# Attention and mixture of experts in one core: a shorter way from quotient to logits, four routing groups instead of five

## The chip, the cores and the metric
The kernel runs on one core of a Trainium2 chip. The metric is the device time of one execution in microseconds. Before the change three runs gave 344.79, 345.01 and 345.48 us, median 345.01. The engines are PE (matrix multiplication), DVE (vector), ACT (scalar), POOL (general purpose, which here also issues the indirect DMAs) and SP (which issues the other DMAs).

## What is computed
A block of two layers on 16 sequences of 256 tokens with 128 channels, all in float32 as far as the result shows:

```python
x = x + attn(layernorm(x))        # causal linear attention, 16 heads of 8: phi(q), phi(k) = elu + 1
#   kv = running sum of k outer v, ksum = running sum of k; y = (q kv) / (q ksum + 1e-6); y @ W_proj + b
x = x + moe(layernorm(x))         # 8 experts, hidden width 512, top 2 of a softmax over x @ Wr + br
#   h = relu(x @ W1[e] + b1[e]); out = h @ W2[e] + b2[e]; mixed with the two normalised gates
```

## The kernel before, in words
**Stages.** First the projections q, k, v of all 16 sequences are made (up to 47.6 us of the profile). Then a loop over s = 0 to 15 makes the attention of one sequence (two tiles of 128 tokens) a step. A last stage runs the experts over 39 blocks of 256 token slots; behind it the rows are gathered, mixed with the gates and stored.

**A step of the loop.** All engines are programmed by hand, each with its own order of instructions, and meet at semaphores. PE makes running sums of k outer v by matrices of ones (`prefix(s+1, 0)` and `prefix(s+1, 1)`), single-buffered in PSUM, so each waits until DVE has multiplied the former content (`multiply`, L923). DVE multiplies by q, reduces over a head (`reduce`, L934) and divides (`quotient`, L942 to L946). PE turns the quotient (`turn_y`, L1305), ACT copies it out (`copy_yT`, L645), PE projects it (`proj`, L1313 to L1317). ACT copies the new x with its sum (`copy_x2`, L651) and makes variance (`statistics(s-1)`); POOL raises it to the power -1/2 (`power_2`, L524); ACT scales x (`norm_2`, L672 to L690); PE turns that (`turn_x2(s-3)`, L1327), ACT copies it (`copy_x2T`, L697), and PE makes the router's logits (`logits(s-3)`, L1337).

**Routing.** Sequences are routed in groups of `GROUPS`. When the logits of a group are complete, DVE chooses the two experts of each token (`choose_first`, `choose_second`, 15 small operations), PE ranks them (`ranks`) and DVE makes `positions`. With these POOL scatters the rows of each half tile to the regions of their experts in DRAM (`scatter_x`, L534, 64 in all); after a block of experts it scatters two outputs (`scatter_y`, L566, 78 in all). After the first three groups (10 sequences) DVE works out a table of blocks (`table_*`), which PE spreads over partitions (`spread`) and DVE copies (`table_copies`, L1083).

**Weights.** Scales of the expert weights are made on DVE (`scales`). ACT casts the weights to a high part in two passes (`cast_weights`, L639, 32 calls), POOL subtracts for the low part (`weights_low`, 16). Tables give how many of these stand in which step: `CASTS` (between the copies, behind them), `LOWS`, `KV_AT` (products of k and v on POOL), `X_AT` (row scatters).

## Time and profile before

| | us |
|---|---|
| median of 3 runs | 345.01 |
| the profiled execution | 345.68 |
| its span | 343.93 |
| PE busy | 289.6 (84%) |
| DVE busy | 275.0 (80%) |
| ACT busy | 224.7 (65%) |
| POOL busy | 248.5 (72%) |
| granted TensorE clock, mean | 0.936 |

Between the profiled execution and the span lie 1.75 us, and the profiled execution is 0.67 us over the median. Busy shares are means over stages with different limits, so the sections below read the stages one by one. The loop's steps are best counted by the start of L946, the last operation of a quotient: it comes once a step.

### The profile page before, as it was taken

The numbers are of one execution on the slowest core, as the hardware profiler recorded it, in microseconds if no ns is written. First come the engines' busy times: TensorE is split into PE (matmuls) and PEld (weight loads), VectorE is DVE, ScalarE is ACT, GpSimd is POOL, SyncE is SP. The second block draws the span as 40 slices with busy tenths as digits, with TensorE's granted clock in tenths as the row PEclk, the third lists the DMA queues.
The fourth block names the chain that finished last, engine by engine and source line by source line (L and its number), as shares of the span: only waits on it lengthen the run. The fifth ranks groups of instructions, "written<-read, shape, count | busy, mean of one in ns | idle before, by whom it ended". The sixth has DMA issues, their size and how long they took to land.

```text
span 343.9 us, 7875 instructions
## 1 busy us (share of the span) xinstructions
PE 289.6 (84%) x2234; PEld 207.3 (60%) x2237; DVE 275.0 (80%) x623; ACT 224.7 (65%) x654; POOL 248.5 (72%) x252
## 2 busy tenths in 40 slices
PE   4798999989989999899695799999999999995000
PEld 4587855545545555555453577688888898884000
DVE  5888899999978987997999279986777777773096
ACT  2588721469989855555408896688888888882091
POOL 4648999659999998877775577777777777777200
PEclk9699999999999999999879699999999999999655
DMA  8991000000000001011110364516445645511497
GB/s 226 352 286 47 0 2 0 0 4 0 1 0 2 0 15 43 31 53 50 42 51 33 78 110 103 104 56 102 110 104 105 117 99 104 98 56 53 134 381 240
DMA packets 50026, 29.16 MB, mean 85 GB/s; under 512 B 34993, under 2 KB 44639, under 8 KB 49986
## 3 DMA queue, kind: packets, MB, share of 16 engines
q1 hardware_dynamic: 45142, 19.02, 22.6%
q0 software_dynamic: 4544, 9.38, 9.4%
q8 instruction: 20, 0.33, 0.4%
q10 hardware_dynamic: 300, 0.27, 0.3%
q14 instruction: 20, 0.16, 0.2%
HBM read 10.87 MB, written 12.67 MB: 68 GB/s over the span
## 4 chain that ended last, share of the span: by engine, by line
PE 43%; DVE 19%; ACT 12%; POOL 10%; issue 10%; DMA 4%; SPq 1%; ACTq 0%; POOLq 0%; DVEq 0%
POOL y_rows L566 10%; PE ps L1286 9%; PE ps L1285 6%; PE ps L1259 4%; DVE nd L934 3%; ACT xs L682 3%; DMA qk<-y_rows 3%; PE ps L1449 2%; PE ps L1261 2%; PE ps L1451 2%; PE ps L1450 2%; PE ps L1468 2%; PE ps L1473 2%; PE ps L1469 2%; ACT junk L661 2%
## 5 line engine op out<-in xcount | busy, mean ns | idle before, releaser
L566 POOL DMA_INDIRECT y_rows<-kvt,yid x78 | 74.7, 957 | 23.8 <-issue 22.3
L534 POOL DMA_INDIRECT x_rows<-rows,pos_i x64 | 62.4, 974 | 21.3 <-issue 17.4
L740 ACT ACTIVATE ps<-ps,b1s 128x256 f32<-128x256 f32 x156 | 60.1, 448 | 16.9 <-PE ps L1451 16.2
L1171 DVE TENSOR_TENSOR wraw<-ps,wraw 128x1024 f16<-128x1024 f32 x39 | 47.8, 1225 | 19.9 <-ACT wraw L746 19.6
L1449 PE MATMUL ps<-wraw,w1h 128*128 128x256 f16 x156 | 43.4, 278 | 0.5 <-issue 0.4
L1451 PE MATMUL ps<-wraw,w1l 128*128 128x256 f16 x156 | 43.1, 276 | 0.0
L1450 PE MATMUL ps<-wraw,w1h 128*128 128x256 f16 x156 | 43.1, 276 | 0.0
L934 DVE TENSOR_REDUCE nd<-work 128x144 f32<-128x1152 f32 x32 | 41.9, 1348 | 0.4
L923 DVE TENSOR_TENSOR work<-ps,qk 128x1024 f32<-128x1024 f32 x32 | 38.1, 1216 | 5.0 <-PE ps L1286 4.9
L1468 PE MATMUL ps<-w,wraw 128*128 x312 | 39.8, 219 | 0.0
L1469 PE MATMUL ps<-w,wraw 128*128 x312 | 39.7, 219 | 0.0
L645 ACT ACTIVATE xT_s<-ps 128x256 f32<-128x256 f32 x16 | 6.1, 381 | 41.2 <-PE ps L1305 41.1
L1468 PEld LDWEIGHTS ps<-w,wraw 128*128 128x128 f16 x312 | 30.1, 97 | 0.9 <-issue 0.2
L1469 PEld LDWEIGHTS ps<-w,wraw 128*128 128x128 f16 x312 | 30.3, 97 | 0.2
L1166 DVE CAST wraw<-ps 128x512 f16<-128x512 f32 x39 | 26.9, 690 | 2.9 <-ACT ps L740 2.6
L746 ACT ACTIVATE wraw<-ps 128x512 f16<-128x512 f32 x39 | 23.3, 597 | 3.6
L505 POOL TENSOR_TENSOR kvt<-qk,v 128x1024 f32<-128x1024 f32 x12 | 25.3, 2135 | 0.0
L1473 PE MATMUL ps<-w,wraw 128*128 x312 | 23.8, 219 | 0.2 <-DVE wraw L1171 0.2
L1286 PE MATMUL ps<-kvt,tri 128*128 128x512 f32 x48 | 23.6, 593 | 0.0
L1259 PE MATMUL ps<-wqkv,xT_s 128*128 128x256 f32 x64 | 20.4, 403 | 0.0
L1449 PEld LDWEIGHTS ps<-wraw,w1h 128*128 x156 | 15.4, 98 | 7.3 <-issue 3.9
L1473 PEld LDWEIGHTS ps<-w,wraw 128*128 128x128 f16 x312 | 19.0, 98 | 0.5 <-DVE wraw L1171 0.4
(250 smaller groups left out, 733.1 us busy)
## 6 DMA issues: line engine op xcount, KB each, us to landing
qk<-y_rows SPq DMA_DIRECT2D x8, 512.0 KB, 6.7
wraw<-in_L_ffn_W_dram SPq DMA_DIRECT2D x1, 2048.0 KB, 11.1
out_dram<-x SPq DMA_DIRECT2D x8, 256.0 KB, 4.3
x<-in_L_attn_x_dram SPq DMA_DIRECT2D x3, 512.0 KB, 7.2
y_rows<-kvt,yid POOLq DMA_INDIRECT x78, 2.8
x_rows<-empty SPq DMA_DIRECT2D x9, 130.0 KB, 2.8
x_rows<-rows,pos_i POOLq DMA_INDIRECT x64, 2.3
wraw<-x_rows SPq DMA_TRANSPOSE x39
```

The lines of the kernel that those rows point to most:

```text
L534: nc.gpsimd.indirect_dma_start(out=x_rows, out_offset=bass.IndirectOffsetOnAxis(ap=pos_i[:, c, t:t + 1], axis=0), in_=rows[:, t, :], in_of ...
L566: nc.gpsimd.indirect_dma_start(out=y_rows, in_=ysb[:, n % YG, g], in_offset=None, out_offset=bass.IndirectOffsetOnAxis(ap=yid[:, n, g:g + ...
L740: ins = nc.scalar.activation(o, o, ACT.Relu, bias=b1s[:, bass.ds(e * HC + c, 1)])
L934: nc.vector.tensor_reduce(nd[:, s % 2, a].rearrange("p (h j) -> p j h", j=NPL), m_s[:, a].rearrange("p (j h i) -> p j h i", j=NPL, i=DH), ...
L1171: nc.vector.tensor_tensor(hl[:, n % HB], inner(n), hh[:, n % HB], ALU.subtract).then_inc(lo_done, 1)
L1286: ins = nc.tensor.matmul(o, tri[:, :], kv[a][:, cols], start=(a == 0), stop=True)
L1449: nc.tensor.matmul(o, wh, xh, start=True, stop=False)
L1450: nc.tensor.matmul(o, wh, xl, start=False, stop=False)
L1451: ins = nc.tensor.matmul(o, wl, xh, start=False, stop=True)
L1468: nc.tensor.matmul(o, h, second_layer(n, c, 0), start=False, stop=False)
L1469: nc.tensor.matmul(o, h, second_layer(n, c, 1), start=False, stop=False)
L1473: ins = nc.tensor.matmul(o, hl[:, n % HB, c, g * P:(g + 1) * P], second_layer(n, c, 0), start=False, stop=(g == GPB - 1 and c == HC - 1))
```

## The change
1. The turn of the normed x, the logits and all that follows come one step earlier: `norm_2(s-1)`, `turn_x2(s-2)`, `logits(s-2)` instead of s-2, s-3, s-3. `turn_x2` now stands behind both prefixes of PE, the logits behind the denominators. ACT copies x2T at the end of its step, ahead of the casts, not at its start.
2. Four groups of 5, 5, 3 and 3 sequences instead of five of 3, 4, 3, 3 and 3. A group is chosen three steps after its last sequence (`ROUTE`) instead of four; group 2, whose like was chosen behind the loop, is chosen in step 15. The table is still of the first 10 sequences and made in steps 12 to 14 instead of 13 to 15.
3. The weights' scales are made in step 0 instead of 1, `bias_scales` in step 1 instead of 2. The casts stand in steps 0, 1 and 3 to 6 (11, 5, 4, 4, 4, 4) instead of 2 to 7 (6 each, then 2).
4. Intermediate values of scales and of the choice lie in PSUM instead of SBUF, and some buffers are shared.

```diff
-    GROUPS = [3, 4, 3, 3, 3]
+    GROUPS = [5, 5, 3, 3]
-    FIRST = 3
+    FIRST = 2
+    ROUTE = 3
+    TABLE_AT = G_LAST[FIRST - 1] + ROUTE
-    CASTS = {**{s: (3, 3) for s in range(2, 7)}, 7: (2, 0)}
-    LOWS = {3: 3, 4: 3, 5: 3, 6: 3, 7: 3, 8: 1}
+    CASTS = {0: (4, 7), 1: (0, 5), 3: (0, 4), 4: (0, 4), 5: (0, 4), 6: (0, 4)}
+    LOWS = {0: 4, 1: 1, 2: 2, 3: 1, 4: 2, 5: 2, 6: 4}
-    KV_AT = {0: (6, 7), 2: (8,), 3: (9,), 4: (10,), 5: (11,), 6: (12,), 7: (13,), 8: (14,), 10: (15,)}
+    KV_AT = {0: (6, 7), 1: (8,), 2: (9,), 3: (10,), 4: (11,), 5: (12,), 6: (13,), 11: (14, 15)}
-    X_AT = {8: 2, 9: 5, 10: 5, 11: 6, 12: 6, 13: 4, 14: 9, 15: 3}
+    X_AT = {7: 5, 8: 5, 9: 5, 10: 5, 12: 8, 13: 6, 14: 6}
+    X_LATE = 2
...
@@ POOL, a step of the loop
-                if s == 2:
-                    pool.wait_ge(scale_done, 1)
-                if s >= 2:
-                    power_2(s - 2)
+                if s >= 1 and s < U - 1:
+                    power_2(s - 1)
...
@@ POOL, behind the loop
+            for n in range(sent, sent + X_LATE):
                 scatter_x(n)
-            last_group = TOP * TPU * G_U0[NG - 1]
             power_2(U - 2)
-            scatter_x(TOP * T1)
+            for n in range(sent + X_LATE, sent + 2 * X_LATE + 1):
+                scatter_x(n)
             power_2(U - 1)
...
@@ ACT, a step of the loop
             for s in range(U):
-                if s >= 3:
-                    copy_x2T(s - 3)
-                if s - 3 in ended_by:
-                    copy_logits(ended_by[s - 3])
                 between, behind = CASTS.get(s, (0, 0))
                 for n in range(cast, cast + between):
                     cast_weights(n)
                 copy_yT(s)
+                if s - 2 in ended_by:
+                    copy_logits(ended_by[s - 2])
                 if s >= 1:
                     statistics(s - 1)
                 copy_x2(s)
...
-                if s >= 2:
-                    norm_2(s - 2)
+                if s >= 1:
+                    norm_2(s - 1)
+                if s == U - 1:
+                    statistics(s)
+                if s >= 1:
+                    copy_x2T(s - 1)
                 for n in range(cast + between, cast + between + behind):
                     cast_weights(n)
...
@@ DVE, a step of the loop
-                if s == 3:
+                if s == 0:
+                    maxima_over_partitions()
+                if s == 1:
+                    bias_scales()
                     second_sides()
-                if s == 1:
-                    maxima_over_partitions()
-                if s - 4 in ended_by:
-                    choose_first(ended_by[s - 4])
-                    choose_second(ended_by[s - 4])
+                if s - ROUTE in ended_by:
+                    choose_first(ended_by[s - ROUTE])
+                    choose_second(ended_by[s - ROUTE])
                 reduce(s, 0)
...
+                if s == 0:
+                    scales()
+                if s == U - 1:
+                    positions(FIRST)
                 reduce(s, 1)
-                if s == U - 1:
+                if s == TABLE_AT + 2:
                     table_copies(0)
                 quotient(s)
...
-                if s >= 3:
-                    split_low(s - 3)
+                if s >= 2:
+                    split_low(s - 2)
...
-            choose_first(FIRST)
-            choose_second(FIRST)
-            positions(FIRST)
-            split_low(U - 3)
             split_low(U - 2)
...
@@ PE, turn_y(u)
-                if u >= 3:
-                    pe.wait_ge(x2T_out, u - 2)
+                if u >= 2:
+                    pe.wait_ge(x2T_out, u - 1)
...
@@ PE, a step of the loop
                 if s + 1 < U:
                     prefix(s + 1, 0)
...
-                if s == U - 1:
+                if s + 1 < U:
+                    prefix(s + 1, 1)
+                if s >= 2:
+                    turn_x2(s - 2)
+                if s == TABLE_AT + 2:
                     pe.wait_ge(x2_done, s)
                     spread(0)
-                if s >= 3:
-                    turn_x2(s - 3)
-                if s + 1 < U:
-                    prefix(s + 1, 1)
-                if s - 4 in ended_by:
-                    ranks(ended_by[s - 4])
-                elif s == U - 1:
-                    pe.wait_ge(table_done, 2)
-                    logits(s - 3)
-                elif s >= 3:
-                    logits(s - 3)
+                if s - ROUTE in ended_by:
+                    ranks(ended_by[s - ROUTE])
                 turn_y(s)
                 if s + 1 < U:
                     prefix_denominators(s + 1)
...
+                if 2 <= s < U - 1:
+                    logits(s - 2)
+                if s - 2 in ended_by:
+                    pe.wait_ge(lg_out, ended_by[s - 2] + 1)
                 proj(s)
...
@@ PE, behind the loop
-            pe.wait_ge(x2T_out, U - 3)
-            ranks(FIRST)
-            pe.wait_ge(rank_out, FIRST + 1)
-            turn_x2(U - 3)
             logits(U - 3)
             turn_x2(U - 2)
             up(0)
```

**On PE, a step without a choice.** Before, from the first prefix of a step to the denominators (xs is the normed x, xsT its turned copy, y_s the quotient):

```order
L1286 MATMUL ps<-kvt,tri 128x512 [waits m_done,kv_done]
L1286 MATMUL ps<-kvt,tri 128x512
L1327 MATMUL ps<-ident,xs 128x128 [waits x2T_out,yT_out,xs_done]
L1327 MATMUL ps<-ident,xs 128x128
L1285 MATMUL ps<-kvt,ones 128x512 [waits m_done,kv_done]
L1286 MATMUL ps<-kvt,tri 128x512
L1285 MATMUL ps<-kvt,ones 128x512
L1286 MATMUL ps<-kvt,tri 128x512
L1337 MATMUL ps<-wr,xsT 128x8 [waits small_in3,x2_done,x2T_out]
L1337 MATMUL ps<-wr,xsT 128x8
L1305 MATMUL ps<-ident,y_s 128x128 [waits x2T_out,yT_out,y_done]
L1305 MATMUL ps<-ident,y_s 128x128
```

With the change the same stretch, up to the logits, reads (L1296 and L1297 are the prefixes, L1338 the turn of x2, L1316 the turn of y, L1350 the logits):

```order
L1297 MATMUL ps<-rows,tri 128x512 [waits m_done,kv_done]
L1297 MATMUL ps<-rows,tri 128x512
L1296 MATMUL ps<-rows,ones 128x512 [waits m_done,kv_done]
L1297 MATMUL ps<-rows,tri 128x512
L1296 MATMUL ps<-rows,ones 128x512
L1297 MATMUL ps<-rows,tri 128x512
L1338 MATMUL ps<-ident,xs 128x128 [waits x2T_out,yT_out,xs_done]
L1338 MATMUL ps<-ident,xs 128x128
L1316 MATMUL ps<-ident,y_s 128x128 [waits x2T_out,yT_out,y_done]
L1316 MATMUL ps<-ident,y_s 128x128
L1305 MATMUL ps<-qk,tri 128x128 [waits y_done,m_done]
L1306 MATMUL ps<-qk,tri 128x128
```

The turn of x2 has moved from between the prefixes to right ahead of the turn of y, and that one's wait on x2T_out is now for ACT's copy of this same x2.

**On ACT, between two steps with casts.** Before, from the last part of a norm to the statistics of the next step (w2 and wraw are the weights, L639 a cast):

```order
L690 ACTIVATE ps<-xs 128x256 [waits xl_done]
L639 ACTIVATE wraw<-wraw,sc 128x512 [waits pfx_done,scale_done]
L639 ACTIVATE w2<-wraw,sc 128x4x128 [waits pfx_done,scale_done]
L639 ACTIVATE wraw<-wraw,sc 128x512 [waits pfx_done,scale_done]
L697 ACTIVATE xsT<-ps 128x256 [waits lg_done,x2T_done]
L639 ACTIVATE w2<-wraw,sc 128x4x128 [waits pfx_done,scale_done]
L639 ACTIVATE wraw<-wraw,sc 128x512 [waits pfx_done,scale_done]
L645 ACTIVATE xT_s<-ps 128x256 [waits proj_done,yT_done]
L657 ACTIVATE mean<-sums 128x2 [waits x2_done]
```

With the change (L701 ends the norm, L708 is the copy of x2T, L647 a cast, L653 the copy of yT):

```order
L701 ACTIVATE ps<-xs 128x256 [waits xl_done]
L708 ACTIVATE xsT<-ps 128x256 [waits lg_done,x2T_done]
L647 ACTIVATE w2<-wraw,sc 128x4x128 [waits pfx_done,scale_done]
L647 ACTIVATE wraw<-wraw,sc 128x512 [waits pfx_done,scale_done]
L647 ACTIVATE w2<-wraw,sc 128x4x128 [waits pfx_done,scale_done]
L647 ACTIVATE wraw<-wraw,sc 128x512 [waits pfx_done,scale_done]
L653 ACTIVATE xT_s<-ps 128x256 [waits proj_done,yT_done]
```

The copy of x2T has moved ahead of all casts that stand between two steps, and four of them lie between it and the copy of yT.

## Rows read from the trace of the kernel before

**Rows 1.** Busy time by stretch: the loop (us, busy of PE, PEld, DVE, ACT, POOL).
```profile
47.56:185.32 137.76, 126.39 (x528) 71.35 (x526) 126.03 (x249) 80.79 (x283) 115.12 (x95) 0.98 0.06 19
```

**Rows 2.** The chain that ended last, one step of it (start, us, what).
```profile
119.32 0.86 PE ps L1285 x2
...
127.46 0.86 PE ps L1285 x2
```

**Rows 3.** Timeline of DVE: the quotients of steps 0, 3, 7, 11 and 15.
```profile
55.56 0.42 DVE L946 TENSOR_TENSOR y_s<-nd,ps 128x256 f32<-128x256 f32 x1
...
79.28 0.42 DVE L946 TENSOR_TENSOR y_s<-nd,ps 128x256 f32<-128x256 f32 x1
...
113.21 0.42 DVE L946 TENSOR_TENSOR y_s<-nd,ps 128x256 f32<-128x256 f32 x1
...
146.87 0.42 DVE L946 TENSOR_TENSOR y_s<-nd,ps 128x256 f32<-128x256 f32 x1
...
184.90 0.42 DVE L946 TENSOR_TENSOR y_s<-nd,ps 128x256 f32<-128x256 f32 x1
```

**Rows 4.** Timeline of PE, from the logits of step 7 to step 8.
```profile
114.45 0.51 PE L1337 MATMUL ps<-wr,xsT 128*128 128x8 f32 x4
114.81 0.41 PE L1305 MATMUL ps<-ident,y_s 128*128 128x128 f32 x2
...
115.74 0.60 PE L1313 MATMUL ps<-x,ident 128*128 128x256 f32 x2
...
116.28 0.61 PE L1317 MATMUL ps<-wproj,xT_s 128*128 128x128 f32 x4
116.73 1.88 PE L1286 MATMUL ps<-rows,tri 128*128 128x512 f32 x4
118.88 0.44 PE L1327 MATMUL ps<-ident,xs 128*128 128x128 f32 x2 [0.27 <-ACT xs L682]
```

**Rows 5.** Timeline of ACT: copy of x2T, casts, copy of yT.
```profile
113.19 0.36 ACT L697 ACTIVATE xsT<-ps 128x256 f32<-128x256 f32 x1
113.45 0.71 ACT L639 ACTIVATE w<-wraw,sc 128x512 f16<-128x512 f32 x1
114.06 0.71 ACT L639 ACTIVATE wraw<-wraw,sc 128x512 f32<-128x512 f32 x1
115.27 0.39 ACT L645 ACTIVATE xT_s<-ps 128x256 f32<-128x256 f32 x1 [0.50 <-PE ps L1305]
```

**Rows 6.** DVE: the products' group with its waits, and one choice's ends.
```profile
L923 DVE TENSOR_TENSOR work<-ps,qk 128x1024 f32<-128x1024 f32 x30 | 35.7, 1216 | 5.0 <-PE ps L1286 4.9
...
132.56 0.22 DVE L983 TENSOR_TENSOR ps<-lg,ps 128x64 f32<-128x64 f32 x1
...
136.37 2.61 DVE L934 TENSOR_REDUCE nd<-work 128x144 f32<-128x1152 f32 x2
```

**Rows 7.** Timelines of PE and DVE around the table.
```profile
171.08 3.75 PE L1286 MATMUL ps<-wraw,tri 128*128 128x512 f32 x4 [2.86 <-DVE work L923]
...
179.46 0.51 PE L1337 MATMUL ps<-wr,xsT 128*128 128x8 f32 x4
...
183.94 0.17 DVE L1083 CAST table_i<-ps 128x26 int32<-128x26 f32 x1
```

**Rows 8.** Timeline of POOL: the 41st row scatter and the last.
```profile
191.52 1.03 POOL L534 DMA_INDIRECT x_rows<-rows,pos_i  x1 [3.15 <-DVE rows L954]
192.58 0.72 POOL L524 TENSOR_TENSOR rstd<-var,neghalf 128x2 f32<-128x2 f32 x1
...
319.85 0.96 POOL L566 DMA_INDIRECT y_rows<-kvt,yid  x1 [0.31 <-issue]
```

**Rows 9.** The reduces of a choice, from PSUM and from SBUF, by form.
```profile
L968 DVE TENSOR_REDUCE r<-ps 128x6 f32<-128x48 f32 x6 | 1.2, 207 | 0.2
L968 DVE TENSOR_REDUCE r<-ps 128x8 f32<-128x64 f32 x2 | 0.5, 225 | 0.1
...
201.60 0.20 DVE L968 TENSOR_REDUCE r<-lg 128x6 f32<-128x48 f32 x1
```

More of the change, by code:

```diff
@@ L211, in block_kernel @@
         ps_br = scratch(E)
+        ps_sc = scratch(10)
         ps_lg = scratch(MOST, E)
-        ps_others = scratch(MOST, E)
         ps_second = scratch(MOST, E)
         ps_xs = ps[:, 5, 0:TPU * D].rearrange("p (a d) -> p a d", a=TPU)
+        ps_wall = ps[:, 6, T + P:T + P + 3]
+        b2s, b2f = (ps[0:E, 5, TPU * D + k * D:TPU * D + (k + 1) * D] for k in range(2))
         def kv_home(u):
@@ L371, in routed @@
         def routed(g, at, n):
-            if g > FIRST or g == FIRST and at >= RANK:
+            if g > FIRST or g == FIRST and at >= COUNT:
                 return ps[:, 6, at:at + n]
@@ L545, in _ @@
             for s in range(U):
-                if s == 2:
-                    pool.wait_ge(scale_done, 1)
-                if s >= 2:
-                    power_2(s - 2)
-                for n in range(low, low + LOWS.get(s, 0)):
+                if s >= 1 and s < U - 1:
+                    power_2(s - 1)
+                for n in range(low, low + LOWS.get(s, 0) if s else 0):
                     weights_low(n)
-                low += LOWS.get(s, 0)
                 for u in KV_AT.get(s, ()):
                     kv_products(u)
-                if s in (5, 10):
-                    token_ids(s // 10)
+                if s == 0:
+                    for n in range(LOWS[0]):
+                        weights_low(n)
+                low += LOWS.get(s, 0)
+                if s in (3, 9):
+                    token_ids(s // 9)
                 for n in range(sent, sent + X_AT.get(s, 0)):
-                    assert G_LAST[in_group[n // TOP // TPU]] + 5 <= s
+                    assert G_LAST[in_group[n // TOP // TPU]] + ROUTE <= s
                     scatter_x(n)
@@ L674, in norm_2 @@
                 act.wait_ge(shift2_done, u + 1)
-                if u == U // 2:
-                    act.wait_ge(pfx_done, 10 * TPU)
+                if u in (0, U // 2):
+                    last = max(w for w in range(U) if KV_HOME[w] == f"rows{u // (U // 2)}")
+                    act.wait_ge(pfx_done, (last + 1) * TPU)
                 if u >= 4:
@@ L754, in copy_y @@
                                      ACT.Copy).then_inc(y_out, 1)
-            statistics(U - 1)
-            copy_x2T(U - 3)
-            norm_2(U - 2)
-            copy_x2T(U - 2)
             norm_2(U - 1)
@@ L885, in scales @@
             def scales():
[L886 removed]
+                piece = lambda a, b: ps_sc[:, a:b]
+                i32 = lambda a, b: ps_sc[:, a:b].bitcast(I32)
                 EXPONENT = 0x7F800000
[L888 to L891 removed]
@@ L898, in scales @@
[L898 to L908 removed]
+                dve.wait_ge(wall_done, 1)
@@ new lines, in scales @@
+                link(nc.vector.tensor_scalar(piece(0, 2), ps_wall[:, 0:2], 1e-18, None, ALU.max))
+                link(nc.vector.tensor_scalar(i32(2, 4), i32(0, 2), EXPONENT, None, ALU.bitwise_and))
+                link(nc.vector.tensor_copy(sc[:, 6:7], ps_wall[:, 2:3]))
+                link(nc.vector.scalar_tensor_tensor(out=piece(4, 5), in0=piece(2, 3), scalar=2.0 * D, in1=sc[:, 6:7],
+                                                    op0=ALU.mult, op1=ALU.add))
+                link(nc.vector.tensor_scalar(i32(5, 6), i32(4, 5), EXPONENT, None, ALU.bitwise_and))
@@ new lines, in scales @@
+                link(nc.vector.reciprocal(piece(6, 7), piece(5, 6)))
+                link(nc.vector.reciprocal(piece(7, 8), piece(3, 4)))
+                link(nc.vector.tensor_scalar(sc[:, 13:14], piece(7, 8), W_TOP, None, ALU.mult))
+                link(nc.vector.tensor_scalar(sc[:, 17:18], piece(6, 7), H_TOP, None, ALU.mult))
+                nc.vector.tensor_scalar(sc[:, 12:13], piece(6, 7), H_TOP / X_SCALE, None, ALU.mult).then_inc(scale_done, 1)
+            def bias_scales():
+                piece = lambda a, b: ps_sc[:, a:b]
+                link(nc.vector.scalar_tensor_tensor(out=piece(8, 9), in0=piece(7, 8), scalar=W_TOP, in1=sc[:, 17:18],
+                                                    op0=ALU.mult, op1=ALU.mult))
+                link(nc.vector.tensor_copy(sc[:, 19:20], piece(8, 9)))
+                link(nc.vector.reciprocal(sc[:, 20:21], piece(8, 9)))
+                dve.wait_ge(small_in[6], 16)
+                link(nc.vector.tensor_scalar(b2s, b2r[:, :], sc[0:E, 19:20], None, ALU.mult))
+                link(nc.vector.tensor_copy(b2hml[:, 0], b2s))
+                link(nc.vector.tensor_tensor(b2f, b2s, b2hml[:, 0], ALU.subtract))
+                link(nc.vector.tensor_copy(b2hml[:, 1], b2f))
+                nc.vector.tensor_tensor(b2hml[:, 2], b2f, b2hml[:, 1], ALU.subtract).then_inc(b2_done, 1)
```

91 lines of the change are left out of this document (36 added, 55 removed).

## The prediction, made before the changed kernel was run
> **What bounds the kernel now.** I read the busy time by stretch first [rows 1]: in the loop over 16 sequences (47.56 to 185.32 us) DVE is busy 126.0 and PE 126.4 of 137.8 us, so either may bind. The chain that ended last and the engines' timelines then say where. Behind the loop it is POOL: from its 41st row scatter (191.52) to the last (319.85) stand 101 pitches and one power_2 [rows 8], which is 1.26 us a scatter and no wait between, and 23.1 us of gather, mix and store follow to the span's 343.93. So the end is the moment at which POOL gets its 41st row scatter, plus a fixed tail. That scatter waits for the positions of group 3, which DVE works out after the loop's last quotient (184.90). So what the loop's last quotient loses or wins goes whole to the end, and the distance from it to the last scatter (319.85 - 184.90 = 134.95 us) is the second term.
>
> Inside the loop the steps take 6.7 us where DVE alone binds, and 8.14 where the chain goes round through PE and ACT (119.32 to 127.46) [rows 2]. PE's own work in such a step [rows 4], start to start: logits 0.36, turn of y (0.26) and denominators (0.67) 0.93, projection 0.54 + 0.45, first prefix 1.72, turn of x2 an estimated 0.28 of its 0.44, second prefix 3.44 (four of 0.86; the chain's first such piece is in [rows 2]): 7.7 us. So PE can't follow DVE's 6.7; it catches up only where DVE makes a choice. DVE waits 5.0 us in all for prefixes, 1.0 in the step shown [rows 6]. A part of it is PE's stop of 0.27 for ACT's xs, ahead of the second prefix.
>
> **The change, part by part.** All steps are counted from quotient to quotient (start of L946) [rows 3]: before has 55.56, then 23.72 for steps 1 to 3, 33.93 for 4 to 7, 33.66 for 8 to 11 and 38.03 for 12 to 15.
>
> *The turn of x2 behind the second prefix.* This takes ACT's xs off the way to the prefix. But the turn of y of step s now waits for x2T_out of s-2, and the turn that feeds it is the instruction right ahead of it; before, 3.44 us of prefix lay between. From start to start: turn 0.44, ACT's copy 0.38, two semaphores of 0.05 make 0.92 instead of 0.27 [rows 4, 5]. So PE's step is 7.7 + 0.65 = 8.35 us, and the way before took 8.14. The hoped-for gain (PE free of the xs wait) is spent at once, and the denominators, behind the turn of y, come 0.7 us late to DVE as well.
>
> *Casts.* ACT now has four casts (0.61 each) between the copy of x2T (s-1) and the copy of yT (s+1), in steps 3 to 6, and the copy of x2T waits for PE's turn behind the second prefix. That closes a ring: projection's last part 0.45, prefixes 5.16, turn 0.44, copy 0.28, casts 2.45, copy of yT 0.38, semaphores 0.1: 9.26 us a step [rows 2, 4, 5]. Before, three casts stood there and PE's second prefix covered them. DVE follows the ring: split_low waits about 1.8 us for xs_beside, whose norm is in the step of ACT that is late. Steps 4 to 6: 3 x 9.26 = 27.8. Step 7 holds the choice of 10 tiles: 6.7 + choice 4.05 (3.81 for 8 tiles [rows 6], and 15 operations by 0.018 for 16 elements more, as the reduce of 48 and of 64 shows, 0.207 and 0.225 [rows 9]) + waits of 1.85 (split_low), 0.7 (denominators) and 1.3 (the copy of logits stands behind casts and copy of yT) = 14.6. Less 0.4 that the first ring finds ready: 42.0 against 33.93, **+8.1 us**.
>
> *Steps 0 to 3.* Step 0 takes the maximum and ten scale operations of 0.2 us: +2.0. Steps 1 to 3 lose them and take one split_low (0.33) earlier: -1.5. Together **+0.5 us**.
>
> *Steps 8 to 11.* They lose a choice (before in step 10). PE starts them caught up by the choice of step 7, so two go at about 7.3 and two at 8.35. Once POOL is late: its last weights_low wait for the casts of step 6, two kv_products stand behind them, and power_2(6) is needed in the same step now, not one later; ACT stands about 4 us and split_low 2.9. 7.3 + 9.6 + 7.3 + 8.35 = 32.5 against 33.66: **-1.2 us**.
>
> *Steps 12 to 15.* Step 12: the larger choice, +0.5, and waits of 0.9 and 0.7 where before had about 1.2 of its 5.0 in that stretch: +0.4. The group that was chosen after the loop is chosen in step 15: 3.81 - 0.26 = 3.55 for 6 tiles, and two operations for its positions, 0.5 in all. And the table is read one step earlier, in step 14, where PE still has two prefixes ahead of spread. The trace prices that [rows 7]: in before PE gets the table step's first product at 171.08 and has the second prefix done at 179.46, for a part at 1.2 GHz (four matmuls take 3.75 us where the step in [rows 4] has 1.88). The same stretch, then turn of y with its wait 0.91, denominators, logits and projection 2.0, prefixes 5.16, turn 0.27 and spread 0.5, comes to 188.3; DVE from the same point is at table_copies after 183.94 - 171.08 = 12.9. It waits some 4.2 us; before it waited nothing, since step 15 has no prefix to make. Sum 0.5 + 0.4 + 4.1 + 4.2 = 9.2, with 0.2 of late denominators: 47.4 against 38.03, **+9.4 us**.
>
> The last quotient so comes 16.8 us late, at 201.7. Walking all engines through both orders with these durations gives 16.2 (and for before a loop of 129.9 us where the trace has 129.3); I take 16.5.
>
> *After the loop.* The 41st scatter needed the choice behind the loop and came 6.6 us after the quotient (191.52). Its positions are now there before the quotient; POOL, still at the scatters of step 14, takes it 1.5 us after. In its stream stands one power_2 more (1.0), a wait for var(15) (0.4), and one of 1.85 for y_out(1), since PE starts its first block 7.4 instead of 8.8 us after the quotient. Last scatter: quotient + 1.5 + 127.6 + 2 x 1.0 + 1.3 = +132.4, against 134.95: **-2.5 us**. PE is not the bound: its last copy of y (316.21, 122.5 after block 0 starts at 193.69) would be 129.9 after the quotient and allow +131.6.
>
> *Into PSUM.* Scale chain and marks move from SBUF to PSUM. The same reduce of 48 takes 0.21 from PSUM and 0.20 from SBUF [rows 9], so I cost it at nothing: 0 to 0.01 x 40 operations = 0.4 us. The Trainium skill, "VectorE: DVE Perf Modes", section on the TRN2 errata, gives 58 cycles of fixed cost from SBUF and 120 from PSUM at 0.96 GHz; by that the sum would be an estimated 2.6 us more for 40 operations. The rows here don't bear that out.
>
> Sum: +16.5 - 2.5 = **+14.0 us** on the profiled 345.68, so 359.7; the median of before is 0.67 lower, so **359.0**.
>
> **Rivals.** (1) *Clock stays up.* The 2.86 us of idle ahead of 171.08 came with the half clock [rows 7]. In after, PE stands about 3 us in step 13. If it doesn't fall, 3 us of the 4.2 of table_copies go, less what then waits for y: 356.7. For it: that idle is at the edge. 15 in 100. (2) *The casts hide*, if ACT is free before PE needs yT: then 8.35 instead of 9.26 for four steps, 355.3. Against it: the waits are in order. 9 in 100. (3) *Faster.* If the turn of y finds x2T ready and ACT keeps up, only DVE binds: the 5.0 us for prefixes [rows 6] go, 1.9 of added DVE work comes (two larger choices, one split_low, positions in the loop), and 2.5 go after the loop: 345.0 - 3.1 - 2.5 = 339.4. It decides where the 0.65 us per step is nought and the four casts don't stand ahead of yT. For it: DVE's work fits; against it: two instructions side by side on PE with ACT between. 6 in 100. (4) *Worse.* power_2 is late in most steps, since it must come between var and norm_2 of one ACT step now and takes 0.72 [rows 8]; if POOL's scatters (1.26 each, five to eight a step) stand ahead of it in steps 8 to 14, another 1 us a step: 366. 8 in 100. (5) *No change* within 0.2% (what a measurement of this kernel can tell): 2 in 100.
>
> **How the numbers follow.** The forecast has 60 in 100, between 357 and 362. With (1) and half of (2) the range reaches down to 354.5, and up to 362.5: 8 in 10. Faster 0.06, same 0.02, slower 0.92.
>
> **What would show it.** Quotients 9 us and more apart in steps 4 to 6, with four casts between copy of x2T and copy of yT; PE idle 0.65 us for x2T at the turn of y in every step; DVE idle of 4 us ahead of table_copies and of over 1 us ahead of split_low; the 41st scatter within 2 us of the last quotient. The forecast is wrong if split_low and the turn of y don't wait, or if DVE's idle in the loop stays near 6 us.

## The result, and the profile after

Four runs of the changed kernel take 363.4 to 366.2 us, median 364.38, beside 344.79 to 345.56 (median 345.25, four runs) for the kernel before: ratio 1.056 (95% interval 1.051 to 1.061). The forecast was 359.0 in a range of 354.5 to 362.5: the right direction and too little of it. The profiled execution took 363.4 us, span 361.7, so in the span the change costs 17.8 us, where the working has 14.0.

The page of the changed kernel, its busy times and the clock in 40 slices. PE, DVE, ACT and POOL do almost the work of before. What is new is idle time, and more of the lower clock around the table and behind the loop: 0.66 in the 20th slice (172 to 181 us), 0.68 and 0.50 in the 23rd and 24th (199 to 217 us). Before, the lowest of these were 0.67 in 171 to 180 us and 0.62 in 189 to 198 us:

```profile
PE 293.0 (81%) x2232; PEld 210.3 (58%) x2235; DVE 275.4 (76%) x606; ACT 226.7 (63%) x653; POOL 248.6 (69%) x252
...
PEclk9899999999999999999699658999999999999755
```

The quotients of steps 0, 3, 7, 11 and 15, for [rows 3]:

```profile
57.48 0.42 DVE L962 TENSOR_TENSOR y_s<-nd,ps 128x256 f32<-128x256 f32 x1
...
79.80 0.42 DVE L962 TENSOR_TENSOR y_s<-nd,ps 128x256 f32<-128x256 f32 x1
...
121.93 0.42 DVE L962 TENSOR_TENSOR y_s<-nd,ps 128x256 f32<-128x256 f32 x1
...
156.16 0.42 DVE L962 TENSOR_TENSOR y_s<-nd,ps 128x256 f32<-128x256 f32 x1
...
204.83 0.42 DVE L962 TENSOR_TENSOR y_s<-nd,ps 128x256 f32<-128x256 f32 x1
```

The same stretches by engine (us, busy of PE, PEld, DVE, ACT, POOL with instructions in brackets, clock). In steps 4 to 7 DVE works 30.9 of 42.1 us and the clock is full, so engines wait for each other there; only behind 121.93 does the clock take part:

```profile
79.80:121.93 42.13, 37.26 (x156) 20.82 (x154) 30.92 (x52) 28.56 (x95) 30.20 (x23) 1.00 0.00 1
121.93:156.16 34.23, 30.57 (x124) 18.29 (x125) 27.38 (x39) 19.74 (x75) 25.73 (x26) 0.95 0.10 32
156.16:204.83 48.67, 34.07 (x152) 19.83 (x150) 40.74 (x100) 18.77 (x73) 33.40 (x31) 0.90 0.09 31
204.83:215.00 10.17, 7.18 (x31) 5.65 (x31) 1.64 (x5) 6.64 (x27) 8.19 (x10) 0.50 0.39 78
```

**The ring, step 6.** Timelines of ACT and PE. Read it round: the turn of x2 (101.58) releases the copy of x2T (102.00), four casts stand behind that, the copy of yT starts only at 104.73, and the projection's last part (105.15) waits for it. PE stands twice, 0.56 us ahead of the turn of y, for the copy of x2T, and 0.55 us for the copy of yT. In [rows 5] the same copy of yT waits for PE instead:

```profile
102.00 0.38 ACT L708 ACTIVATE xsT<-ps 128x256 f32<-128x256 f32 x1 [1.91 <-PE ps L1338]
102.28 0.71 ACT L647 ACTIVATE w<-wraw,sc 128x512 f16<-128x512 f32 x1
...
104.73 0.36 ACT L653 ACTIVATE xT_s<-ps 128x256 f32<-128x256 f32 x1
```
```profile
101.58 0.38 PE L1338 MATMUL ps<-ident,xs 128*128 128x128 f32 x2
102.53 0.41 PE L1316 MATMUL ps<-ident,y_s 128*128 128x128 f32 x2 [0.56 <-ACT xsT L708]
...
105.15 0.71 PE L1328 MATMUL ps<-wproj,xT_s 128*128 128x128 f32 x4 [0.55 <-ACT xT_s L653]
```

**Behind the last casts, steps 9 and 10.** POOL's last `weights_low` and the two products of k and v behind it (`kv_products(13)`) end at 129.4. ACT has waited 4.00 us for rstd, PE stands 1.38 us ahead of its turn of x2 and 0.68 us ahead of the turn of y. From 134.07 on its matmuls take 1.20 and 1.06 us instead of 0.68 and 0.61, up to 138.45:

```profile
130.15 0.48 ACT L680 ACTIVATE shift<-rstd,mean 128x1 f32<-128x1 f32 x2 [4.00 <-POOL rstd L529]
```
```profile
131.59 0.44 PE L1338 MATMUL ps<-ident,xs 128*128 128x128 f32 x2 [1.38 <-ACT xs L691]
132.71 0.41 PE L1316 MATMUL ps<-ident,y_s 128*128 128x128 f32 x2 [0.68 <-ACT xsT L708]
...
134.07 1.20 PE L1324 MATMUL ps<-x,ident 128*128 128x256 f32 x2
...
136.13 2.48 PE L1297 MATMUL ps<-wraw,tri 128*128 128x512 f32 x4
138.45 1.02 PE L1296 MATMUL ps<-wraw,ones 128*128 128x512 f32 x2
```

**Step 13.** `split_low(s)` is the DVE operation that subtracts the high part of the normed rows of sequence s from the rows themselves. For s below `SIDED` = 10 it reads the rows from a copy that ACT puts into PSUM, from there on from SBUF. DVE's `split_low(10)` takes 2.24 us where its neighbours take 0.42. It ends at 172.23; POOL's products, `kv_products(14)` and `(15)` one behind the other, end at 171.94. PE then waits 4.45 us and comes back at half clock; before, it waited 2.86 at this place [rows 7]. In step 14 DVE waits 3.91 us for the spread:

```profile
169.99 2.24 DVE L970 TENSOR_TENSOR rows<-xs,rows 128x256 f16<-128x256 f32 x1
...
193.27 0.18 DVE L1100 CAST table_i<-ps 128x26 int32<-128x26 f32 x1 [3.91 <-PE ps L1376]
```
```profile
167.73 4.21 POOL L510 TENSOR_TENSOR wraw<-qk,v 128x1024 f32<-128x1024 f32 x2
...
206.41 0.96 POOL L539 DMA_INDIRECT x_rows<-rows,pos_i  x1 [0.30 <-issue]
...
337.78 0.95 POOL L572 DMA_INDIRECT y_rows<-kvt,yid  x1 [0.30 <-issue]
```
```profile
176.34 3.75 PE L1297 MATMUL ps<-v,tri 128*128 128x512 f32 x4 [4.45 <-DVE work L939]
```

The last two rows of POOL are the 41st scatter, 1.6 us behind the last quotient, and the last one, 132.95 behind it; [rows 8] has 6.6 and 134.95.

### The profile page after: what moved, and what is told of

Same layout as the page of the kernel before. It is cut to its first block, busy times and chain, and to the rows that moved or that the text cites. A ratio compares the mean times of both kernels' runs of the same rounds, so it can differ in the third digit from the quotient of the medians.

```text
span 361.7 us, 7851 instructions
## 1 busy us (share of the span) xinstructions
PE 293.0 (81%) x2232; PEld 210.3 (58%) x2235; DVE 275.4 (76%) x606; ACT 226.7 (63%) x653; POOL 248.6 (69%) x252
## 3 DMA queue, kind: packets, MB, share of 16 engines
q0 software_dynamic: 4544, 9.38, 9.1%
## 4 chain that ended last, share of the span: by engine, by line
PE 42%; DVE 24%; issue 12%; POOL 12%; ACT 7%; DMA 2%; ACTq 0%; POOLq 0%; DVEq 0%; SPq 0%
PE ps L1297 11%; POOL y_rows L572 8%; PE ps L1296 5%; PE ps L1270 3%; PE ps L1460 2%; DVE nd L950 2%; DVE work L939 2%; PE ps L1462 2%; PE ps L1461 2%; PE ps L1484 2%; DVE x L1231 2%; PE ps L1479 2%; PE ps L1480 2%; ACT wraw L647 2%; POOL x_rows L539 2%
## 5 line engine op out<-in xcount | busy, mean ns | idle before, releaser
L1460 PE MATMUL ps<-wraw,w1h 128*128 128x256 f16 x156 | 43.9, 281 | 1.1 <-issue 0.6
L1461 PE MATMUL ps<-wraw,w1h 128*128 128x256 f16 x156 | 43.7, 280 | 0.0
L1479 PEld LDWEIGHTS ps<-w,wraw 128*128 128x128 f16 x312 | 30.2, 97 | 0.9 <-issue 0.2
L1480 PEld LDWEIGHTS ps<-w,wraw 128*128 128x128 f16 x312 | 30.4, 97 | 0.2
L529 POOL TENSOR_TENSOR rstd<-var,neghalf 128x2 f32<-128x2 f32 x16 | 11.5, 720 | 26.9 <-ACT var L673 26.9
L708 ACT ACTIVATE xsT<-ps 128x256 f32<-128x256 f32 x16 | 6.1, 381 | 37.4 <-PE ps L1338 37.3
L1297 PE MATMUL ps<-kvt,tri 128*128 128x512 f32 x48 | 23.6, 594 | 0.0
```

The source lines that it names most:

```text
L1297: ins = nc.tensor.matmul(o, tri[:, :], kv[a][:, cols], start=(a == 0), stop=True)
L1460: nc.tensor.matmul(o, wh, xh, start=True, stop=False)
L1461: nc.tensor.matmul(o, wh, xl, start=False, stop=False)
L1479: nc.tensor.matmul(o, h, second_layer(n, c, 0), start=False, stop=False)
L1480: nc.tensor.matmul(o, h, second_layer(n, c, 1), start=False, stop=False)
```

## The experiments

All times by stage are differences of quotients in the profiled execution of each kernel; the tail is the last scatter minus the last quotient. Medians and intervals are those of all comparable runs against the kernel before on the same chip, which had 345.1 to 345.5. There is one trace a kernel, so a clock that stays low longer in that one execution shows in its stages too.

| kernel | 1-3 | 4-7 | 8-11 | 12-15 | tail | median | ratio (95%) |
|---|---|---|---|---|---|---|---|
| before | 23.72 | 33.93 | 33.66 | 38.03 | 134.95 | 345.25 | |
| changed | 22.32 | 42.13 | 34.23 | 48.67 | 132.95 | 364.38 | 1.051-1.061 |
| E1 SIDED 12 | 22.33 | 42.11 | 35.88 | 48.85 | 134.46 | 363.98 | 1.048-1.056 |
| E2 casts first | 22.32 | 39.50 | 30.74 | 47.64 | 132.71 | 356.29 | 1.028-1.035 |
| E3 turn between | 22.66 | 36.78 | 34.01 | 47.62 | 133.16 | 357.43 | 1.029-1.041 |
| E4 before, turn moved | 23.70 | 34.79 | 34.91 | 39.00 | 135.33 | 347.52 | 1.004-1.007 |
| E5 = E2, products moved | 22.33 | 39.51 | 30.74 | 45.89 | 134.15 | 355.73 | 1.029-1.034 |
| E6 = E2, table later | 22.32 | 39.51 | 30.74 | 44.87 | 133.51 | 353.43 | 1.020-1.025 |
| E7 turn inside | 21.98 | 35.14 | 30.44 | 46.89 | 133.77 | 351.10 | 1.014-1.019 |
| E8 all of it | 21.98 | 35.15 | 28.90 | 42.96 | 132.73 | 343.97 | 0.996-0.999 |
| E9 products 13 later | 22.33 | 42.12 | 33.57 | 48.03 | 132.67 | 362.04 | 1.045-1.050 |
| E10 = E8, choice behind | 21.97 | 35.17 | 28.92 | 39.05 | 134.87 | 343.27 | 0.993-0.996 |
| E11 = E8, stops filled | 21.97 | 35.15 | 28.92 | 42.97 | 133.15 | 345.00 | 0.998-1.0005 |
| E13 = E10, products back | 21.97 | 35.16 | 28.90 | 40.07 | 134.60 | 343.47 | 0.994-0.997 |
| E14 = E10 again | 21.99 | 35.14 | 28.90 | 39.03 | 134.78 | 343.09 | 0.993-0.996 |

**E1, split_low out of PSUM.**

```diff
-    SIDED = 10
+    SIDED = 12
```

> The changed kernel with SIDED 12 instead of 10: the split_low of sequences 10 and 11 read PSUM instead of xs in SBUF, for two more copies on ScalarE (0.37 us each). Theory: split_low(10) took 2.24 us instead of 0.42 because it reads and writes SBUF while GpSimd's kv_products(14, 15) do the same; from PSUM it takes about 0.4 to 1 us and the kernel's 364.4 fall by 1.5 to 3 us, the stop of TensorE ahead of step 14 (4.45 us) shortens by as much. Rival: the long operation does not count, since its engine would have waited for the spread anyway: time within 0.7 us of 364.4, and the wait ahead of table_copies grows from 3.9 by what split_low loses.

The time is that of the rival (363.98), the reason is neither's: the wait ahead of table_copies is 3.91 us, as in the changed kernel. split_low(10) now takes 0.42 us, and the next operation takes over the stall:

```profile
171.65 0.42 DVE L970 TENSOR_TENSOR rows<-ps,rows 128x256 f16<-128x256 f32 x1
171.99 1.65 DVE L1041 TENSOR_SCALAR cnt_i<-cnt 128x8 int32<-128x8 f32 x1
```

It is a 128x8 operation from SBUF to SBUF, and it ends at 173.64, 0.03 us behind POOL's product (173.61). So not the operation is slow; it stands until the product is done.

The trace of E1 shows one thing more. Its edit first counts in step 11, and up to step 9 its quotients are those of the changed kernel within 0.06 us. PE's stops are the same too (1.36 and 0.68 us). But the half clock comes at once and lasts to 139.64, and step 10 takes 10.64 us instead of 8.99:

```profile
132.69 0.64 PE L1316 MATMUL ps<-ident,y_s 128*128 128x128 f32 x2 [0.68 <-ACT xsT L708]
...
137.17 3.07 PE L1297 MATMUL ps<-wraw,tri 128*128 128x512 f32 x4
```

The mean clock from 131.6 to 141.0 us is 0.64 here and 0.82 in the changed kernel. The clock is the only difference that the profiles show there, so with the same program it goes with 1.65 us of step 10. This trace is of the longest of E1's four runs (366.7 us), so its steps 8 to 11 (35.88) are no effect of the edit.

**E2, the casts ahead of the copy of x2T, from step 3 on.**

```diff
-                if s >= 1:
-                    copy_x2T(s - 1)
                 for n in range(cast + between, cast + between + behind):
                     cast_weights(n)
+                if s >= 1:
+                    copy_x2T(s - 1)
```

> The changed kernel with ScalarE's four casts of steps 3 to 6 ahead of the copy of x2T instead of behind it, where TensorE's prefixes cover them. Theory (the ring prefixes - turn of x2 - copy - four casts - copy of yT): steps 4 to 7 fall from 42.1 to about 39.2, power_2(6) is no longer late, steps 8 to 11 fall from 34.2 to about 30.5, together 5 to 7 us: 358 to 359.5. Rival (the casts were covered, the cost is the turn of y right behind the turn of x2): no more than 1 us less, 363.5.

8.1 us faster, at 356.3 more than the 358 to 359.5 expected. Both stages come out as worked out (39.50 for 39.2, 30.74 for 30.5), and the casts now lie under PE's prefixes: ACT even waits for both turns. Another 1.0 us of the gain is in steps 12 to 15, where the clock in 171 to 181 us is 0.88 instead of 0.69. By steps, only 6, 7, 9 and 10 of those from 4 to 11 gain: steps 4 and 5 take 9.88 and 8.45 us, as in the changed kernel (9.88 and 8.50), so their length does not come from the casts.

```profile
101.17 0.38 ACT L708 ACTIVATE xsT<-ps 128x256 f32<-128x256 f32 x1 [0.26 <-PE ps L1342]
102.15 0.38 ACT L653 ACTIVATE xT_s<-ps 128x256 f32<-128x256 f32 x1 [0.59 <-PE ps L1320]
```

**E3, the turn of x2 between the prefixes.**

```diff
-                if s + 1 < U:
-                    prefix(s + 1, 1)
                 if s >= 2:
                     turn_x2(s - 2)
+                if s + 1 < U:
+                    prefix(s + 1, 1)
```

> The changed kernel with the turn of x2 of s-2 between the two prefixes, where the kernel before has it (its own of s-3). Theory: the 0.65 us that TensorE stands at each turn of y go, and with them the ring with the casts, which the second prefix now covers: steps 4 to 7 fall from 42.1 to about 37; against it TensorE waits for ScalarE's xs ahead of the second prefix; in all 2 to 4 us less, 360.5 to 362.5. Rival (xs of s-2 comes too late in every step, so that the second prefix is late by 1 us a step): 364 to 370.

6.9 us faster, more than expected. Steps 4 to 7 fall to 36.78: steps 4 to 6, with casts, are 8.19 us each, as are steps 10 and 11 without (8.20 and 8.19), close to the 8.14 of [rows 2]. But where rstd is late, PE now stands ahead of a prefix that DVE needs, so steps 8 to 11 keep their 34 us:

```profile
123.73 0.59 PE L1338 MATMUL ps<-ident,xs 128*128 128x128 f32 x2 [2.30 <-ACT xs L691]
```

**E4, this one part of the change, put into the kernel before.**

```diff
-                if s >= 3:
-                    turn_x2(s - 3)
                 if s + 1 < U:
                     prefix(s + 1, 1)
+                if s >= 3:
+                    turn_x2(s - 3)
```

> The kernel before with one part of the change alone: its turn of x2 (s-3) moved behind the second prefix, right ahead of ranks and logits. Theory of the prediction: turn of y does not wait for this x2T here (it needs that of s-2 steps earlier), but the logits right behind the turn wait for ScalarE's copy, 0.6 us a step of TensorE time where TensorE binds: about 2 us more, 347 to 347.8. Rival (TensorE gains 0.27 a step from not waiting for xs): 343 to 345.

347.52, 2.1 us slower: the first theory. (The stages in the table are of the longest of its seven runs, 349.5 us, and overstate it.) PE's wait has moved from xs to the copy of xsT right behind the turn, as here ahead of the logits:

```profile
123.76 0.38 PE L1327 MATMUL ps<-ident,xs 128*128 128x128 f32 x2
124.61 0.61 PE L1337 MATMUL ps<-wr,xsT 128*128 128x8 f32 x4 [0.47 <-ACT xsT L697]
```

**E5, E2 with POOL's last products apart and earlier.**

```diff
-    KV_AT = {..., 11: (14, 15)}
-    X_AT = {7: 5, 8: 5, 9: 5, 10: 5, 12: 8, 13: 6, 14: 6}
+    KV_AT = {..., 9: (14,), 10: (15,)}
+    X_AT = {7: 5, 8: 5, 9: 3, 10: 2, 11: 5, 12: 8, 13: 6, 14: 6}
```

> The kernel with casts first (356.3 us) with GpSimd's kv_products(14) in step 9 and (15) in step 10 instead of both in step 11, and the row scatters of those steps spread to make room (3, 2, 5 instead of 5, 5, 0 in steps 9, 10, 11). The first experiment on this moved the long operation instead of removing it: with split_low(10) out of PSUM (0.42 us) the table's first operation in SBUF behind it took 1.65 us and ended with GpSimd's product. Theory now: a VectorE operation from SBUF to SBUF of this kind stands until GpSimd's product is done, so the product has to go from beside the table's operations; step 13 then takes 10.2 instead of 12.1 us and the kernel 1.9 to 3.5 us less: 353 to 354.5. Rival: another operation meets the product wherever it stands, or GpSimd's power_2 comes late in steps 9 to 11: 355.6 or more.

The loop does what the theory said: split_low(10) 0.43 us, step 13 10.25 instead of 12.11. The median does not: 0.6 us less, which is in the rival's range. In the profile the tail takes back 1.4 of it. Behind the last quotient the clock is 0.50 for 16 us here, in E2 for 10 us only, and POOL waits 2.42 us for its first y instead of 1.25. E2 and E5 were measured on different chips, and the runs of E5 have mean clocks of 0.909 to 0.938, those of E2 0.928 to 0.942. E12 to E14 took this up again.

**E6, E2 with the table one step later.** `table_full` to `table_pick` in step 13, `table_start` to `table_diag` in 14, spread and `table_copies` in 15: in each condition `TABLE_AT + k` becomes `TABLE_AT + k + 1`.

> The kernel with casts first (356.3 us) with the table's operations one step later each (steps 13, 14, 15 instead of 12, 13, 14), as the kernel before has them, so that TensorE's spread stands in step 15, which has no prefix to make. Theory: the wait of some 4 us ahead of table_copies goes, TensorE's stop in step 13 is shared out over two steps and its clock stays up, so steps 12 to 15 fall from 47.6 to about 43, and the last scatter is 0.5 to 1 us nearer to the quotient: 351 to 352.5. Rival: the table's operations only move, step 15 has the choice of group 2 besides and becomes longer by what step 14 loses: 355.5 or more.

2.9 us faster, a little less than expected. The wait ahead of table_copies is gone, and step 14 falls from 12.19 to 9.87, step 13 from 12.11 to 9.28. Step 15 grows from 10.58 to 13.00, since DVE's 2.4 us of table_start to table_diag now stand in it beside the choice.

**E7, the changed kernel with the turn of x2 inside the second prefix.** `prefix(s + 1, 1)` calls it between its two halves:

```diff
                 for g in range(2):
+                    if g == 1 and inside is not None:
+                        turn_x2(inside)
                     o = ps[:, 2 * a + g, :]
```

> The changed kernel with the turn of x2 (s-2) between the two halves of the second prefix: behind its two matmuls into the one bank, ahead of the two into the other. There TensorE has 1.72 us more for ScalarE's xs than between the prefixes, and ScalarE has 1.72 us for its copy before the turn of y. Theory (the two waits of 0.65 and 0.27 us and the ring with the casts are the whole loss of steps 4 to 11): TensorE's step is its own work, 7.7 us; steps 4 to 7 about 35.2 instead of 42.1, steps 8 to 11 about 30.6 instead of 34.2, in all 353.5 to 355.5. Rival (the casts bind by ScalarE's or GpSimd's own work, whatever stands around them): 357 or more, as in the kernels with casts first or with the turn between the prefixes.

351.10, 13.3 us faster than the changed kernel with the same casts at the same place, and 2.4 us below the range expected. Steps 4 to 7 (35.14 for 35.2) and 8 to 11 (30.44 for 30.6) are as worked out; steps 5 and 6 take 7.70 and 7.69 us, PE's own work. Moving one pair of instructions by 1.72 us of matmuls takes away both of PE's waits and the ring.

**E8, all parts.** E7, E5's products, E6's table, and the last casts spread:

```diff
-    CASTS = {0: (4, 7), 1: (0, 5), 3: (0, 4), 4: (0, 4), 5: (0, 4), 6: (0, 4)}
-    LOWS = {0: 4, 1: 1, 2: 2, 3: 1, 4: 2, 5: 2, 6: 4}
+    CASTS = {0: (4, 7), 1: (0, 5), 3: (0, 4), 4: (0, 4), 5: (0, 4), 6: (0, 2), 7: (0, 2)}
+    LOWS = {0: 4, 1: 1, 2: 2, 3: 1, 4: 2, 5: 2, 6: 2, 7: 1, 8: 1}
```

> The changed kernel with the turn of x2 inside the second prefix, kv_products(14) and (15) in steps 9 and 10, the table one step later, and the last casts spread over one step more (4, 4, 4, 2, 2 in steps 3 to 7, weights_low to step 8). Theory: the parts add up, since each takes away a wait of its own: loop of 128 to 130 us against 129.3 of the kernel before, last scatter 132 to 133 behind the last quotient against 134.95: 341.5 to 344.5, faster than both. Rival (DVE's own work, with a choice more in the loop, binds, or GpSimd's power_2 is late): 346 to 349.

343.97: the parts add up, and the kernel is 1.1 us faster than the one before (interval 0.996 to 0.999). The loop is 128.99 us, 129.34 before.

**E9, the changed kernel with `kv_products(13)` in step 7.** `KV_AT` has `7: (13,)` for `6: (13,)`.

> The changed kernel (364.4 us) with GpSimd's kv_products(13) in step 7 instead of step 6, so that power_2(6) stands behind the last weights_low only, not behind 4.2 us of products too. Casts and turn of x2 stay as they are. Theory: in steps 8 to 11 the wait of ScalarE and VectorE for the late rstd (4.00 and 2.8 us, at 130) and TensorE's two stops with a falling clock behind it are what makes 34.2 us of 30.7 (the value with the casts first); power_2(6) now comes 4.2 us earlier, so 1 to 3 us go, all of them between the quotients of steps 7 and 11: 361.5 to 363.4. Rival (the four casts of step 6 themselves, ahead of the copy of yT, hold step 8 up; GpSimd's lateness is covered by them): 364 or more.

2.3 us less in the median, inside the expectation. ACT's wait for that rstd is 0.30 instead of 4.00, and the clock of the stretch is 1.00 instead of 0.95. But the profile's steps 8 to 11 fall by 0.7 only, since POOL is late in step 10 instead (10.56 us). So lateness on POOL is moved by this, not removed, and the 0.7 is its worth in one trace. Steps 12 to 15 are 0.6 shorter in it, which the edit does not explain. All four runs have a mean clock of 0.934, those of the changed kernel 0.897 to 0.926.

**E10, E8 with the choice of group 2 back behind the loop.** Calls of `choose_first`, `choose_second`, `positions` and `ranks` for group 2 stand behind the loop, and `power_2(U - 2)` ahead of the late scatters.

> The best kernel so far (343.97 us) with the choice of group 2 and its positions back behind the loop, as the kernel before has them (power_2 of the last sequences then stands ahead of the late scatters). The prediction costed this move at +4.1 us in the loop and -2.5 behind it, a loss of 1.6. Theory (those two terms are right): loop 125.3 instead of 129.0, last scatter 135 to 136.5 behind the last quotient instead of 132.7: 341.5 to 343.7, a gain of 0.3 to 2.5. Rival (behind the loop the choice costs as much as in it, since TensorE's first block and GpSimd's 41st scatter wait for it): 344 to 346.

Loop 125.11 (expected 125.3), tail 134.87 (135 to 136.5), median 343.27: the move into the loop cost 3.9 and gave 2.1 in the profile. This and E14 are the fastest kernels here, 0.6% below the kernel before.

**E11, E8 with PE's stops filled.** 14 transposes ahead of `turn_x2(13)`, 24 ahead of `turn_y(15)`:

```diff
+                    for _ in range(24):
+                        nc.tensor.transpose(ps[:, 5, 0:P], ident[:, :], ident[:, :])
```

> The best kernel so far (343.97 us) with work on TensorE that no one reads in the two long stops of step 15: 14 transposes of the identity into a bank that is free ahead of the turn of x2(13), 24 ahead of the turn of y(15). It measures what the lower clock costs: in the profile of that kernel the clock is 0.50 from the last quotient to 9.4 us behind it, the first up takes 2.5 us instead of 1.3, and GpSimd waits 1.2 and 1.6 us for the first two blocks' y. Theory (the stops bring the clock down): clock near 1 in that stretch, those two waits go in part, 1 to 2.5 us less: 341.5 to 343. Rival (GpSimd's scatters bind behind the loop whatever TensorE's clock): 343.7 to 344.3; and if the added transposes stand in TensorE's way: 344.5 to 346.

345.00 us, by the ratios 0.1% over E8: the expected gain did not come. The number is in the range of the second rival, but the transposes do not stand in the way: the last quotient is where it was (loop 129.01 us, 128.99 in E8). In the profile the half clock comes later rather than not at all: in the 9.4 us behind the last quotient it is 0.68 instead of 0.50, and from 195 to 205 us 0.58 instead of 0.77. The filled stops end at 185.9, and a stop behind them that I had not filled, 2.50 us for ACT's xs, stands right ahead of the experts. What the clock costs there is not measured by this run.

```profile
181.74 4.34 PE L1412 MATMUL ps<-ident 128*128 128x128 f32 x24
...
190.48 0.69 PE L1340 MATMUL ps<-ident,xs 128*128 128x128 f32 x2 [2.50 <-ACT xs L691]
```

**E12 to E14, the price of the products beside DVE, on a steadier kernel.** E10 with `11: (14, 15)` and the old `X_AT` (E12, and E13 again), and E10 itself beside E13 on the same chip (E14).

> The best kernel (343.27 us) with one part of it undone: kv_products(14) and (15) stand in step 11 again, as in the changed kernel, and the scatters with them. It measures once more, where runs scatter less, what that part is worth; with the casts first it took 1.75 us out of the loop but only 0.6 out of the median. Theory (a VectorE operation from SBUF to SBUF stands until GpSimd's product ends): split_low(10) takes 2 to 3 us and ends with the product, the step behind quotient 12 grows from 7.46 by 1 to 2 us, the median by as much: 344.3 to 345.3. Rival (the time comes back elsewhere, since the step behind is TensorE's): step 13 grows, the loop does not: 343 to 343.8.

> The best kernel with kv_products(14) and (15) back in step 11, once more: in the run before, the kernel before took 409.5 us itself, so that run says nothing on the difference; its trace has split_low(10) at 2.23 us, ended 0.29 us behind the product. Theory as before: the stall is in the loop, between the quotients of steps 12 and 13 (7.46 without it), and is passed on to the median: 344.3 to 345.3 on a chip where the best kernel has 343.3. Rival (TensorE is what step 13 waits for, so the stall is covered in part): 343 to 343.8.

> The best kernel again, beside the one before on the same chip: the difference of the two is the price of the products beside VectorE's operations. Theory: 343.3 again, within 0.5, and 1 to 2 us below its neighbour. Rival: within 0.5 us of its neighbour.

E12 took 403.97 us on a chip where the kernel before took 409.54 in the same minutes, with a tail of 186.2 us; only its split_low is used (2.23 us). E13 has 343.47 (343.41 to 343.81), E14 343.09 (342.83 to 343.28): 0.4 us. The stall is there in full (2.34 us, ended 0.36 behind the product), and step 13 is 9.38 instead of 7.47. But step 12 is 11.54 instead of 12.48: in E14 the moved products make POOL's rstd late there, ACT waits 2.05 us for it (0.36 in E13) and DVE's `split_low(9)` 1.73 us (in E13 it does not wait). The tail is 0.2 shorter. The rivals' numbers hold, their mechanism (TensorE covers the stall) does not: step 13 grows by the whole 1.9 us, and the loop by 1.0. From first quotient to last scatter the two traces differ by 0.86 us. The medians differ by less because, in the traces at least, E14 has its first quotient 0.47 us later, where both kernels have the same program (E10, the same kernel as E14, has it 0.95 earlier than E14). So moving the products is worth 0.4 us by the medians and 0.9 by the traces.

```profile
155.39 2.34 DVE L968 TENSOR_TENSOR rows<-xs,rows 128x256 f16<-128x256 f32 x1
```
```profile
153.16 4.21 POOL L510 TENSOR_TENSOR wraw<-qk,v 128x1024 f32<-128x1024 f32 x2
```

And from E14, `split_low(9)` behind the late rstd:

```profile
145.36 0.42 DVE L968 TENSOR_TENSOR rows<-ps,rows 128x256 f16<-128x256 f32 x1 [1.73 <-ACT ps L699]
```

## Why the prediction was right in kind and too small

| step of it | forecast | profile |
|---|---|---|
| Steps 0 to 3 | +0.5 | +0.5 |
| Steps 4 to 7 | +8.1 | +8.2 |
| Steps 8 to 11 | -1.2 | +0.6 |
| Steps 12 to 15 | +9.4 | +10.6 |
| last quotient | +16.5 taken (sum 16.8) | +19.9 |
| After the loop | -2.5 | -2.0 |
| behind the last scatter | 0 | -0.2 |
| span | +14.0 | +17.8 |

**Turn of x2 and casts.** Right in mechanism, and right in the sum of steps 4 to 7 partly by luck. PE stands 5.8 us in ten of the turns of y for x2T, 0.56 us in most, where I had 0.65 in every one. The quotients of steps 4 to 6 are 9.88, 8.50 and 9.23 apart, where I had 9.26 for each and "9 us and more" as the sign. Only step 6 is the ring: in E2, where the casts are out of it, step 6 falls to 8.46 and step 7 from 14.52 to 12.71, and steps 4 and 5 stay. Step 5 is PE's step without the casts (8.35 forecast, 8.45 in E2). Step 4, as I read the rows, pays back what PE lost before it: steps 1 to 3 went at 8.94, 6.35 and 7.03, and PE turned the y of step 0 0.5 us behind its quotient, that of step 3 5.0 us behind (84.81 after 79.80). In E7, where PE's step is shorter, step 4 takes 8.00. So the ring binds only from step 6 on, and PE's lag, which was not in the sum, made up for the rest. E2 breaks the ring on ACT, E3 and E7 on PE, and E4 alone shows what the turn's place costs in the kernel before, 2.1 us; there it is the logits that wait. "The casts hide" was wrong as a rival for the changed kernel, and E7 shows its condition: they hide at the same place in the order as soon as the turn comes 1.7 us earlier.

**Steps 8 to 11 is a step that failed.** 7.3 and 9.6 for steps 8 and 9 were right (7.26, 9.53), 8.35 for step 11 nearly (8.45). Step 10 was put at 7.3 and took 8.99. I had assumed that PE catches up behind the late power_2. E2, without that lateness, has 8.31 there, so some 1.0 us is PE's own step at once. The rest of about 0.7 goes with the slower matmuls behind its stops of 1.38 and 0.68 us. That the clock can do this, the trace of E1 shows: the same program up to there, with the lower clock right behind the stops, took 1.65 us more in this step. How much of just this 0.7 is the clock stays argued; E9, where the clock stays at 1.00, moved the lateness too.

**Steps 12 to 15 is the other.** The waits were right: 3.91 us for the spread against 4.2, and E6 gives back 2.8 of these steps. What was not in the sum is split_low(10), costed at 0.42 and taking 2.24, and the longer stop of PE that follows (4.45 us). E5 takes 1.75 us out of these steps by moving the products. For the time of the kernel E13 and E14 put it at 0.4 us in the medians and 0.9 in the traces, so in their arrangement the stall of 1.9 us counts in part.

**After the loop.** The 41st scatter comes 1.6 us behind the quotient, as forecast (1.5). POOL waits 2.9 us for the first two y instead of 1.85, and 0.45 near the end; each of these holds the 0.3 us that stand ahead of any scatter. The wait of 0.4 for var(15) did not come. The working names waits of 0.4 and 1.85 and adds 1.3 for them; with their sum the term would have been -1.6 instead of -2.5, so its nearness to -2.0 is no proof of it.

**Into PSUM** cost nothing: the same reduce of 48 takes 0.206 to 0.208 us from PSUM in the changed kernel, 0.203 from SBUF, and the first quotient comes 1.9 us later for the forecast 2.0 of scale work. The 2.6 us estimated from the Trainium skill, "VectorE: DVE Perf Modes", TRN2 errata, did not come.

**Spread.** The 1.3 us between +17.8 in the span and +19.1 in the medians are that the profiled execution was the fastest of four, 1.0 below their median, and that the one before was 0.4 above its own. The four runs have mean clocks of 0.926, 0.926, 0.897 and 0.925, and the one at 0.897 is the longest (366.2), as in E1 (366.7 at 0.897). My range took in no such spread.

## What to carry to other kernels

An instruction that turns a buffer for another engine wants independent work on both sides of it: ahead of it for its input, behind it for its copy; at the edge of a block of work it gets one of the two. Moving work off the path into the slack of an engine also moves it behind waits that this engine has, so draw the whole ring with what stands in order on the helper. And where two engines can hold each other up at memory, look at what runs beside each small operation, also when busy shares are low.
